# A fused attention and mixture-of-adapters block on one NeuronCore: the order of ScalarE's and VectorE's work at the head of a steady step

## The reference

```
h  = layernorm(x)
q, k, v = h @ wq.T + bq, h @ wk.T + bk, h @ wv.T + bv      # each as 32 heads x 32
s  = einsum('bshd,bstd->bsht', q, k) / sqrt(32)             # heads against heads, within one row
x1 = x + einsum('bsht,bstd->bshd', softmax(s), v)
n  = layernorm(x1)
g  = top-2 of 8 experts by n @ gate_w.T, softmax over the two
out = x1 + n @ base_w.T + base_b + 2 * sum over experts e of g[e] * (n @ A[e].T @ B[e].T)
```

## Time and profile before

| | |
|---|---|
| median of 3 runs | 1276.71 us (1274.11 to 1278.17) |
| the profiled execution | 1278.39 us |
| its span | 1275.3 us |
| TensorE's mean granted clock over the span | 0.997 of full speed |
| busy: PE / DVE / ACT / POOL | 1242.0 / 1067.5 / 743.3 / 426.5 us |
| PE's share of the chain that ended last | 84% |
| the mean traffic of the DMA queues | 107 GB/s |

### The profile page before, as it was taken

One profiled execution on the slowest core, in us unless ns is written; L12 is line 12 of the kernel. 1 busy time (PEld: TensorE's weight loads), 2 busy tenths in 40 slices (PEclk: granted clock), 3 DMA queues, 4 the chain that ended last, 5 costly groups with the idle time before them and its releaser, 6 DMA issues.

```text
span 1275.3 us, 30571 instructions
## 1 busy us (share of the span) xinstructions
PE 1242.0 (97%) x12314; PEld 642.1 (50%) x12314; DVE 1067.5 (84%) x1492; ACT 743.3 (58%) x1149; POOL 426.5 (33%) x340
## 2 busy tenths in 40 slices
PE   6899989999999999999999999999999999999998
PEld 4554445455554545455454555545455555545454
DVE  5799898888888888888888888888888888888886
ACT  4876646665556666555666655566665556666431
POOL 0113433334423333442333344233334423333320
PEclk9999999999999999999999999999999999999999
DMA  9823543344444334444433444443344444333330
GB/s 367 295 67 85 133 100 92 89 101 115 101 96 97 96 84 101 115 101 97 97 96 84 102 115 101 97 96 96 84 103 115 99 98 96 96 84 87 85 84 33
DMA packets 295447, 136.41 MB, mean 107 GB/s; under 512 B 265072, under 2 KB 266096, under 8 KB 295408
## 3 DMA queue, kind: packets, MB, share of 16 engines
q1 hardware_dynamic: 228688, 112.28, 33.6%
q10 hardware_dynamic: 66720, 23.60, 7.8%
HBM read 86.03 MB, written 33.03 MB: 93 GB/s over the span
## 4 chain that ended last, share of the span: by engine, by line
PE 84%; DVE 7%; DMA 3%; issue 2%; ACT 2%; SPq 1%; POOL 0%; DVEq 0%; ACTq 0%
PE acc L1630 23%; PE dense_acc L1790 23%; PE acc L1639 22%; PE attn_ps L1732 7%; PE dense_acc L1800 2%; DMA work<-wT_dram 2%; PE low_ps L1769 1%; PE low_ps L1762 1%; PE low_ps L1763 1%; PE dense_acc L1805 1%; DMA turn_dram<-x_turned 1%; DVE w_lo_k L1059 1%; ACT work L401 1%; DVE work L1196 1%; DVE work L1157 1%
## 5 line engine op out<-in xcount | busy, mean ns | idle before, releaser
L1790 PE MATMUL dense_acc<-base_parts,x 128*128 128x512 f16 x1488 | 331.2, 380 | 1.1 <-issue 1.0
L401 ACT COPY work<-work 32x512 f16<-32x512 f16 x498 | 306.5, 615 | 12.4 <-PE attn_ps L1732 0.3
L1790 PEld LDWEIGHTS dense_acc<-base_parts,x 128*128 128x128 f16 x1488 | 145.7, 99 | 165.6 <-issue 2.2
L632 POOL TENSOR_TENSOR work<-work 128x1024 f16<-128x1024 f32 x32 | 68.4, 2137 | 225.9 <-ACT work L917 225.9
L1196 DVE SCALAR_TENSOR_TENSOR work<-acc,acc_to_a,biases_sb 128x512 f32<-128x512 f32 x192 | 136.3, 738 | 1.8
L582 POOL TENSOR_TENSOR columns<-columns 128x1 f32<-128x1 f32 x31 | 9.1, 293 | 362.9 <-ACT work L797 362.9
L763 ACT CAST x_hi<-x_turned 128x1024 f16<-128x1024 f32 x31 | 32.4, 1044 | 155.3 <-PE acc L1639 154.4
L1630 PE MATMUL acc<-w_hi_k,x_hi 128*128 128x512 f16 x496 | 117.5, 380 | 1.6 <-issue 1.6
L1630 PE MATMUL acc<-v_parts,x_hi 128*128 128x512 f16 x496 | 117.5, 380 | 0.0
L1639 PE MATMUL acc<-w_hi_k,x_lo 128*128 128x512 f16 x496 | 117.2, 379 | 0.0
L1630 PE MATMUL acc<-w_hi_q,x_hi 128*128 128x512 f16 x496 | 117.2, 379 | 0.0
(11 more groups left out here) (217 smaller groups left out, 2070.1 us busy)
## 6 DMA issues: line engine op xcount, KB each, us to landing
work<-x_dram SPq DMA_DIRECT2D x64, 512.0 KB, 3.6
work<-work SPq DMA_DIRECT2D x256, 64.0 KB, 2.0
work<-x_dram SPq DMA_DIRECT2D x124, 128.0 KB, 3.8
out_dram<-work SPq DMA_DIRECT2D x31, 512.0 KB, 2.6
x_turned<-turn_dram ACTq DMA_DIRECT2D x30, 512.0 KB, 3.3
work<-wT_dram SPq DMA_DIRECT2D x16, 512.0 KB, 9.9
turn_dram<-x_turned SPq DMA_DIRECT2D x64, 128.0 KB, 3.9
turn_dram<-x_turned ACTq DMA_DIRECT2D x60, 128.0 KB, 4.4
```

What stands on the lines that cost most here:

```text
L401: copy(diag[c * QD:(c + 1) * QD, :, c, j::NQ, :], src).then_inc(vdiag_ready, 1)
L632: nc.gpsimd.tensor_tensor(v_parts_t[:, :, 1, :], turned3, v_parts_t[:, :, 0, :], ALU.subtract).then_inc(v_lo_ready, 1)
L1790: nc.tensor.matmul(dense_acc[n][:, :], rows_part[:, k, :], w_part[:, k, cols], start=(k == 0 and m == 0), stop=False)
```

## The change

Two lists are put in another order; no instruction is added or removed, and no wait is.

- ACT, in steps 3 to 30 (step 2 and the last have orders of their own): the first group of v's copies, half of the second, and the exponentials come ahead of `x2_high(t - 1)`; the other half of the second group and the third follow it.
- DVE, in steps 3 to 30: `shift(t)` comes ahead of the two `finish` operations, and `turn_quads(t + 2)` comes behind k's two biases rather than behind `shift`. The last step keeps its order.

```diff
@@ ACT, step(t) @@
                 else:
+                    spread(t, (0,))
+                    spread_v(nc.scalar.copy, 1, range(NQ // 2))
+                    exponentials(t)
                     x2_high(t - 1)
-                    spread(t, (0,))
-                    exponentials(t)
-                    spread(t, (1, 2))
+                    spread_v(nc.scalar.copy, 1, range(NQ // 2, NQ))
+                    spread(t, (2,))
                     probabilities_high(t)
                     spread(t, (3,))
@@ DVE, step(t) @@
+                if not tile(t, 1):
+                    finish(t - 2, 0)
+                    finish(t - 2, 1)
+                    shift(t)
+                    return last_step(t)
+                shift(t)
                 finish(t - 2, 0)
                 finish(t - 2, 1)
-                shift(t)
-                if tile(t, 2):
-                    turn_quads(t + 2)
-                if not tile(t, 1):
-                    return last_step(t)
                 sum_exponentials(t)
                 probabilities(t)
 
                 dve.wait_ge(vt_ready, t + 1)
                 add_bias(t + 1, 0, FIRST, 0, a_acc, a_biased)
                 add_bias(t + 1, 1, FIRST, 1, a_acc, a_biased)
+                if tile(t, 2):
+                    turn_quads(t + 2)
                 probabilities_low(t)
                 turn_first(t + 1)
```

## The result

| | before | after |
|---|---|---|
| median (4 runs each) | 1277.15 us (1274.11 to 1278.17) | 1365.55 us (1364.5 to 1367.57) |
| ratio | 1 | 1.0698 (95% interval 1.0682 to 1.0714) |
| span of the profiled execution | 1275.3 us | 1362.3 us |

A forecast was written before the change was run, and what follows sets the result against it. TensorE, never idle in steady steps, was taken to bound the kernel; a closed chain with two holds makes steps 40.5 us for 37.22, 27 x 3.28 + 1 − 0.2 = 89 us more, so 1366 us, range 1312 to 1382.

The forecast's parts named there:

- What bounds the kernel: TensorE never idles in a steady step of 37.22 us, so reordering other engines can lengthen a step but not shorten it.
- VectorE's part: Output additions fill the wait for the exponentials, 0; turning the next rows behind k's biases adds 1.17 us to the chain.
- ScalarE's exponentials later by 1.22 us: Six copies now come first on ScalarE, so the exponentials start at 609.85, 1.22 us later than before.
- First hold: GpSimd's x2 low part holds VectorE's rescaling, which ends at 9.34 instead of 7.88 from the first copy: 1.46 us a step.
- Second hold: GpSimd's q low part starts 0.14 us ahead of VectorE's normalisation of x1 and holds it: 2.53 for 0.81, 1.72 us.
- The context's turning: On VectorE, 17.42 us behind the first copy, 19.0 by the step's clock where before 16.95: 2.05 us late.
- TensorE's first wait: TensorE waits for k's first bias, ending at 12.84 where matmuls could begin at 11.83: with the semaphore about 1.05 us.
- TensorE idle about 3.3 us a step: Sign of being right: TensorE idle about 3.3 us in each step, first before the second half of q's matmuls.
- The hold taken literally: Rival: each held VectorE operation runs its whole length behind GpSimd's; 3.68 us a step, 1377 us; 3%.
- One hold only: Rival: the normalisation gets in before q's low part, which stretches instead; 38.8 us a step, 1320 us; 15%.
- Not slower: Rival: x2's low part doesn't hold the rescaling; without both holds 3 us in all, 1280 us, or none; 8%.
- The clock: Rival: TensorE's granted clock falls each step because of its waits; 4.5 us a step, 1398 us; 5%.

The follow-up runs named there:

- e1_vector_only: VectorE's new order alone, ScalarE in the old order, against the kernel before: 1277.44 us, ratio 1.0005.
- e3_no_hold_norm: The changed kernel plus one GpSimd wait from step 3 on: q's low part waits for the normalisation of x1. 1317.97 us, ratio 1.0316.
- e5_no_holds: Changed kernel plus three GpSimd waits from step 3: x2's low part for rescaling, output bias for probabilities' low part, q's low part for normalisation. 1282.27 us.
- e2_scalar_only: The kernel before with ScalarE's half of the change alone, VectorE in the old order: 1440.75 us, ratio 1.1285.
- e7_x2high_first: The changed kernel with x2's high part put back to the head of ScalarE's order: 1382.66 us, ratio 1.0821.
- e4_no_hold_rescale: Changed kernel plus two GpSimd waits from step 3: x2's low part for the rescaling, output bias addition for the probabilities' low part. 1329.61 us.
- e6_x2low_late: The changed kernel plus one GpSimd wait from step 3 on: x2's low part waits for the rescaling. 1352.29 us, ratio 1.0579.

## Why the prediction was right

The forecast was 1366 us, the median is 1365.55. That they meet within half a microsecond is partly luck: the step was put 0.07 us too long, 1.9 us over 27 steps, the profiled spans differ by 87.0 us and not 89, and the four runs of the kernel before spread over 4 us. The mechanism is what held. By its own steps:

- **What bounds the kernel.** That TensorE is never idle in a steady step, so that reordering can only lose, is contradicted by no run: the one kernel below 1277 us gained in step 2 and not in a steady step.
- **VectorE's part: 0 for the output additions, 1.17 us on the chain for the turning.** The additions fit into the wait: VectorE still stands 1.39 us for the exponentials behind them. From the turning to the next operation it is 653.34 − 652.18 = 1.16 us. That the same turning is free while the chain has its gap is what the steady steps of `e1_vector_only` show. No engine waits for the rows that are loaded later, as forecast.
- **ScalarE's exponentials later by 1.22 us.** They start at 644.33, 5.59 of the step's clock, 1.39 later than before. The 0.17 over the forecast is the first copy, which stands behind v's low part as forecast and starts at 1.74 of the step's clock for 1.58.
- **First hold, 1.46 us.** Mis-sized by 0.14: the rescaling is held for 1.32 us (2.545 for 1.224), and `e3_no_hold_norm` against `e5_no_holds` gives 35.7 us for it, 1.3 a step. Its end lies 1.08 us behind GpSimd's, as in rows 7. The term that was off is the start of x2's high part: put at 3.84 + 1.17 = 5.01 behind the first copy, it came at 645.38 − 640.48 = 4.90. I had taken the distance from the exponentials to a copy of v for the one to x2's high part, which is 1.05 us. So GpSimd is done 0.12 us sooner.
- **Second hold, 1.72 us.** 2.54 for 0.81, and 47.6 us in `e3_no_hold_norm`. The 0.14 us by which GpSimd is ahead is in the trace to the hundredth (666.06 and 666.20), and ScalarE's part of q was ready 0.27 us before GpSimd began, where the forecast gave its margin as some 0.3.
- **The context's turning** starts 657.84 − 640.48 = 17.36 us behind the first copy, for 17.42; the normalisation 25.72 for 25.77, x1's low part at 28.18 for 28.22.
- **TensorE's first wait, 1.05 us.** The second half of q starts at 651.67, 12.93 for 11.83: 1.10.
- **TensorE idle about 3.3 us a step.** This sign reads lower, 0.93 + 1.17 + 0.54 = 2.64 us. The profile counts the end of the last matmul before each gap as busy, 0.17 us by the first gap (a delay of 1.10 us, 0.93 of it idle). With that added for all three gaps it is, as an estimate, 3.15 us of the 3.21 by which the step is longer.
- **The step, 40.5.** 40.43. The sum, 89; 88.4 between the medians.
- **The hold taken literally** (3.68 us a step, 1377 us) is out: all held operations end less than their own length behind GpSimd's, 1.08 for 1.22 and 0.55 for 0.81.
- **One hold only** (1320 us) did not happen by itself; `e3_no_hold_norm` made it, with 1318.
- **Not slower** (1280 us) did not happen; `e5_no_holds` made it, with 1282.
- **The clock** stayed at 1.00 through the steady steps' waits of 0.5 to 1.2 us. It is a true danger of such changes, though, as `e2_scalar_only` shows.

## What to carry to other kernels

Where one engine is full, ask of every reordering of the others how much room each hand-over has, and whether a chain that runs from one step into the next has lost its last gap: then each delay on it is paid in every step. List the operations of VectorE and GpSimd that can't run side by side, and look at who asks first at each meeting; a move by a microsecond on a third engine can turn all of them around, and a wait placed on GpSimd, which has time, gives it back. Halves of a change need not add: here one half costs nothing that the medians show, the other 164 us, and both together 88.

## What the runs showed of the hardware

- VectorE and GpSimd stand for each other in more pairs than those before the change showed: the rescaling by x2's low part (2.55 us for 1.22), the low part of the probabilities by the bias addition (1.98 for 1.18), x1's low part by q's low part (3.17 for 1.22, `e1_vector_only`), GpSimd's bias addition by the rescaling (3.34 for 2.36). The pair of rows 7, the rescaling by the bias addition, came back in `e7_x2high_first` (2.70). In each of these cases where VectorE's operation has two SBUF inputs it ended 1.08 us behind GpSimd's, 0.14 us sooner than the 1.22 us that it takes by itself (0.10 for the low part of the probabilities); I have no run that says why.
- A lead of 0.09 us is enough to hold the other for 1.7 us (`e4_no_hold_rescale`). Below 0.04 us the starts in the trace don't tell who stands: q's low part starts 0.03 us ahead of x1's low part both in step 3 of `e1_vector_only` (218.96 and 218.99), where VectorE stood, and in step 3 of the kernel before (221.10 and 221.13), where GpSimd did (3.23 us for 2.12). So a forecast that leaves two operations that close has to keep both outcomes.
- TensorE's granted clock was at 0.50 behind a wait of 3.87 us that returned in each step (`e2_scalar_only`), and back at 1.00 some 3 to 6 us after TensorE had resumed. The cost differed from step to step, 1.3 to 2.9 us. Behind a wait of 2.42 to 2.45 us in step 2 it fell in five traces and stayed at 1.00 in two. Waits of up to 1.8 us in the steps of `e6_x2low_late` left the clock at 1.00.
